# Corner weights multiplied into gathered rows: VectorE instructions of 128 elements in place of 384

## The chip, the cores and the metric

The kernel runs on one core of one Trainium2 chip. The metric is the device time of one execution in microseconds (us). The kernel before took 9420.3 us, the median of 3 runs (9414.35 to 9424.11).

## The reference, cut to what matters

Eight images of 56 x 56 places with 128 channels go through two layers. The first is a deformable convolution: for every place, 4 channel groups and 9 taps, a bilinear sample of the projected image is read at a place that depends on the data. Four corners are each multiplied by a weight, and the taps are added up:

```
def corner(yf, xf, wgt):
    valid = (yf >= 0) & (yf < H) & (xf >= 0) & (xf < W)
    idx = jnp.clip(yf, 0, H - 1).astype(jnp.int32) * W + jnp.clip(xf, 0, W - 1).astype(jnp.int32)
    v = jax.vmap(lambda im, i: im[i])(img, idx)
    return v * (wgt * valid)[..., None]
...
samp = samp.reshape(N, GROUP, H, W, P, Cg)
return jnp.einsum('nghwpc,nhwgp->nhwgc', samp, mask_sm).reshape(N, H, W, C)
```

A projection, two layer norms and an MLP follow. The second layer is an attention with additive scores, `sum(tanh(f_i + g_j + b1) * w2)`, over all earlier places j of each place i, and then a mixture of 64 experts, each of which takes 8 tokens of an image. Everything is float32.

## The kernel before

**Tiling.** An image has 3136 places. They are sampled in 49 tiles of 64 places. A tile uses 128 partitions: 64 places by two halves of the channel groups. A partition then holds two groups of 9 taps, 18 samples (`SAMPLES`), each of 32 channels by 4 corners, 128 float32 numbers. Two tiles make a block of 128 places, of which an image has 25, and a block goes through the projection, the MLP and the attention.

**Gathers.** GpSimd does nothing but issue the gathers. For each tile it issues 18 indirect DMAs, one for each sample (L1223); each reads 128 row numbers from the SBUF tensor `index` and fetches 128 rows of 512 bytes from the tensor `patches` in HBM into one of 4 slots of `gathered`. Before a tile's first gather it waits until the last user of the slot has been summed (`sampled`), which is the tile 4, or at an image's end 3, tiles earlier.

**Weighing and summing.** VectorE waits for a tile's 18 gathers (`gather_done`) and multiplies the slot in place by the corner weights in the step "weigh" (L1405). This step is called a train below. Then comes the step "sample", one reduction of 2304 elements into 64 (L1414), which frees the slot:

```
for lo in range(0, SAMPLES, PIECE):
    part = product[:, lo:lo + PIECE]
    v.tensor_tensor(part, part, weight[:, lo:lo + PIECE].unsqueeze(2)
                    .to_broadcast([P, PIECE, CG, 4]), ALU.mult)
settle()
```

`settle()` (L1242) is a drain of VectorE. Within a train there is none between the multiplications.

**The rest of a block.** After two tiles TensorE and VectorE turn, project and normalize the block ("mix", "mlp_out", "norm", L1271 to L1304, L1427, L1438, L1445), which ends in its keys (L1458 to L1461). ScalarE then computes the tanh of its scores (L1721), 16 rows at a time against up to 1024 earlier places. A block's tanh work grows with its number in the image. TensorE sums the scores (L1891), ScalarE takes the exponentials (L1731), VectorE masks them (L1471) and copies the turned weights (L1482). The weighing and all of this lie in one `pool_mem` tensor or in tensors of their own in SBUF.

**Order.** The order of the steps on TensorE, VectorE, ScalarE and the SP queue is written by a list scheduler when the kernel is built. It works with fixed costs of the steps (`LASTS`, in which "weigh" has 3.2), which do not depend on `PIECE`. Images overlap: the front of the next image and the attention of the present one are interleaved. The last image's order also takes in the experts' work.

Of the kernel before, what the change touches and what calls it, by code (L numbers as in the profile page):

```python
# [34 lines left out]
HID = 512  # L35
EPS = 1e-5
GATHER_SLOTS = 4
PIECE = 3
X1_SLOTS = 10
TANH_COLUMNS = 10240  # L40
PLACES = 4
# [682 lines left out]
def network(nc, io, x2_d, xln2_d, logits_d, patches_d, chosen_d, expert_d, out, images):  # L724
    with ExitStack() as ctx:
# [511 lines left out]
        def _(dve):  # L1237
            v = nc.vector

            def settle():  # L1240

                return v.drain()  # L1242
# [64 lines left out]
            def task(n, odd, name):  # L1307
# [88 lines left out]
                elif what == "weigh":  # L1396
# [5 lines left out]
                    weight = corner_w[:, g, tt].rearrange("p (j k) -> p j k", k=4)  # L1402
# [5 lines that stand above are left out]
# [764 lines left out]
```

How the kernel before makes its waits and increments, by code:

```python
            def task(n, odd, name):  # L1040
                what, i = (*name, 0)[:2]
                b = i % 2
                if what == "image_in":
                    sp.wait_ge(band_turned.sem, band_turned.free(n, i, 2))
                    sp.dma_start(x_band[:, b], io["x"][bass.ds(n * S + i * BAND, BAND), :]
                                 .rearrange("(q p) c -> p q c", p=112)).then_inc(x_band_in[b].sem, 16)
                elif what == "patches":
                    sp.wait_ge(patch_ready.sem, patch_ready.after(n, i))
                    if i < 2 and not (isinstance(n, int) and n == 0):
                        sp.wait_ge(sampled.sem, sampled.after(n - 1, -1))
# [4 lines left out]
                        return  # L1057
                    sp.dma_start(patches_d[int(odd)][i * P:i * P + patch_rows(i), :],
                                 patch[:patch_rows(i), b].rearrange("p g c k -> p (g c k)")).then_inc(patches_out[b].sem, 16)
                elif what == "x_in":
                    sp.wait_ge(mid_ready.sem, mid_ready.free(n, i, 2))
                    sp.dma_start(x_tok[:blk_rows(i), b], io["x"][bass.ds(n * S + i * P, blk_rows(i)), :])\
                        .then_inc(x_tok_in[b].sem, 16)
                elif what == "route":
                    r = blk_rows(i)
                    sp.wait_ge(ln2_ready.sem, ln2_ready.after(n, i))
                    sp.dma_start(x2_d[bass.ds(n * S + i * P, r), :], x2[:r, b]).then_inc(block_out[b].sem, 16)
```

## Time and profile before

| | |
|---|---|
| median of 3 runs | 9420.3 us (9414.35 to 9424.11) |
| span of the profiled execution, first to last instruction | 9429.1 us |
| mean granted TensorE clock | 0.821 of full speed |
| GpSimd busy | 6834.3 us, 7060 instructions |
| ScalarE busy | 6717.5 us, 8200 instructions |
| TensorE matmul busy | 6306.7 us |
| VectorE busy | 6031.0 us, 17780 instructions |
| multiplications by corner weights (L1405) | 2352 instructions, 1141.7 us busy |

Busy time counts an engine's compute instructions alone, so time in which GpSimd's sequencer prepares the next gather is not in it. PE is TensorE, PEld its weight loads, DVE VectorE, ACT ScalarE, POOL GpSimd; a q behind a name means the engine's sequencer (waits, drains, semaphores). A shape such as 128x384 is partitions by elements. The span of the profiled execution is 8.8 us (0.09%) above the median of the runs.

### The profile page before, as it was taken

How to read it: one execution, taken by the hardware profiler on the slowest of the kernel's cores; microseconds unless marked ns; L12 is line 12 of the kernel's file. 1: busy time of each engine (PE TensorE's matmuls, PEld its weight loads, DVE VectorE, ACT ScalarE, POOL GpSimd, SP SyncE). 2: the span in 40 equal slices, each digit the busy share in tenths (PEclk: the TensorE clock that was granted, in tenths of full speed). 3: DMA queues.
4: the chain of work that ended last, by engine and by line, in shares of the span. 5: the costliest groups of instructions: out<-in, count | busy, mean ns of one | idle time of the engine just before them, and what ended most of it. 6: DMA issues, size and time to landing. Idle time of an engine off the chain costs nothing.

```text
span 9429.1 us, 151169 instructions
## 1 busy us (share of the span) xinstructions
PE 6306.7 (67%) x44945; PEld 3370.3 (36%) x44945; DVE 6031.0 (64%) x17780; ACT 6717.5 (71%) x8200; POOL 6834.3 (72%) x7060
## 2 busy tenths in 40 slices
PE   5556666667766767666666676666676666657786
PEld 3233333333333333333333333333333333333444
DVE  6666666665676666766666666666567666776642
ACT  1368965688756887578866798567875688757891
POOL 5777777777777777777777777777777777777730
PEclk7678887888878888788888888878888888878896
DMA  2222222222222222222222222222222222334535
GB/s 86 70 76 57 58 60 63 84 58 58 62 71 76 58 59 62 74 73 57 59 63 78 67 57 62 62 83 60 57 62 69 78 57 69 97 95 134 151 111 187
DMA packets 453930, 711.90 MB, mean 75 GB/s; under 512 B 146576, under 2 KB 261136, under 8 KB 451472
## 3 DMA queue, kind: packets, MB, share of 16 engines
q0 software_dynamic: 225792, 462.87, 18.4%
q1 hardware_dynamic: 227312, 239.17, 8.0%
q8 instruction: 377, 6.18, 0.3%
q14 instruction: 449, 3.68, 0.1%
HBM read 595.51 MB, written 105.96 MB: 74 GB/s over the span
## 4 chain that ended last, share of the span: by engine, by line
POOL 66%; issue 22%; ACT 4%; DVE 3%; PE 2%; DMA 2%; DVEq 1%; SPq 0%; POOLq 0%; ACTq 0%
POOL pool_mem L1223 66%; ACT tanh L1721 3%; DVE pool_mem L1405 1%; DVEq L1242 1%; PE score_ps L1891 1%; DVE y L1414 1%; PE side_ps L2003 0%; DMA pool_mem<-in_weight 0%; DMA pool_mem<-patches_odd,pool_mem 0%; DMA pool_mem<-patches_even,pool_mem 0%; ACT expo L1731 0%; DMA expert_d<-pool_mem 0%; DVE newton L1276 0%; DVE pool_mem L1337 0%; SPq L1174 0%
## 5 line engine op out<-in xcount | busy, mean ns | idle before, releaser
L1721 ACT ACTIVATE tanh<-key_rep,query 128x896 f32<-128x896 f32 (+7 forms) x6400 | 5530.0, 951 | 1457.6 <-DVEq L1242 978.6
L1223 POOL DMA_INDIRECT pool_mem<-patches_even,pool_mem x3528 | 3414.7, 968 | 1146.5 <-issue 1072.4
L1223 POOL DMA_INDIRECT pool_mem<-patches_odd,pool_mem x3528 | 3419.4, 969 | 1075.7 <-issue 1071.7
L1891 PE MATMUL score_ps<-tanh,score_w 128*32 128x512 f32 (+3 forms) x24320 | 2931.5, 596 | 478.2 <-ACT tanh L1721 474.6
L1405 DVE TENSOR_TENSOR pool_mem<-pool_mem 128x384 f32<-128x384 f32 x2352 | 1141.7, 553 | 1334.3 <-DMA pool_mem<-patches_even,pool_mem 699.2
L1891 PEld LDWEIGHTS score_ps<-tanh,score_w 128*32 128x32 f32 x24320 | 745.9, 120 | 2087.2 <-issue 1386.1
L1414 DVE TENSOR_REDUCE y<-pool_mem 128x64 f32<-128x2304 f32 x392 | 999.6, 2550 | 33.1 <-issue 9.8
L1920 PE MATMUL value_ps<-values,expoT 128*128 128x129 f32 (+1 forms) x5200 | 908.4, 324 | 83.9 <-DVE expoT L1482 71.9
L1920 PEld LDWEIGHTS value_ps<-values,expoT 128*128 128x128 f32 (+1 forms) x5200 | 802.3, 228 | 160.7 <-DVE expoT L1482 100.7
L1276 DVE SCALAR_TENSOR_TENSOR newton<-rstd,newton 128x1 f32<-128x1 f32 (+1 forms) x2403 | 529.2, 220 | 188.1 <-issue 9.8
L1790 PE MATMUL turn_ps<-ident,expo 128*128 128x128 f32 (+1 forms) x2632 | 527.6, 323 | 152.7 <-DVE expoT L1482 128.3
L1482 DVE COPY expoT<-turn_ps 128x512 f32<-128x512 f32 (+4 forms) x800 | 455.8, 571 | 201.1 <-PE turn_ps L1790 116.0
L1731 ACT ACTIVATE expo<-score_ps,tiny 128x896 f32<-128x896 f32 (+9 forms) x416 | 383.0, 921 | 276.5 <-PE score_ps L1891 249.1
L1790 PE MATMUL chain_ps<-ident,values 128*128 128x128 f32 (+1 forms) x200 | 79.3, 396 | 730.2 <-DVE values L1445 729.4
L1278 DVE SCALAR_TENSOR_TENSOR rstd<-newton,rstd 128x1 f32<-128x1 f32 (+1 forms) x2403 | 387.8, 161 | 216.4 <-issue 26.7
L1790 PEld LDWEIGHTS turn_ps<-ident,expo 128*128 128x128 f32 (+1 forms) x2632 | 369.5, 168 | 257.1 <-DVE expoT L1482 141.6
L1821 PE MATMUL side_ps<-pool_mem,early 128*128 128x448 f32 x1008 | 427.7, 581 | 30.1 <-DVEq L1242 30.1
L1731 ACT ACT_TABLE_LOAD x198 | 254.0, 1283 | 223.8 <-PE score_ps L1891 218.6
L1867 PE MATMUL chain_ps<-w_fc,hid 128*128 128x128 f32 (+1 forms) x1600 | 250.0, 304 | 163.6 <-ACT hid L1706 163.3
L1860 PE MATMUL chain_ps<-chainT,w_fc 128*128 128x128 f32 (+1 forms) x1600 | 269.3, 320 | 119.4 <-DVE chainT L1433 117.5
L1706 ACT ACTIVATE hid<-chain_ps,b_hid 128x128 f32<-128x128 f32 (+1 forms) x800 | 226.4, 365 | 166.5 <-PE chain_ps L1860 158.4
L1790 PEld LDWEIGHTS chain_ps<-ident,values 128*128 128x128 f32 (+1 forms) x200 | 32.2, 161 | 847.6 <-DVE values L1445 815.7
(168 smaller groups left out, 6035.9 us busy)
## 6 DMA issues: line engine op xcount, KB each, us to landing
pool_mem<-in_weight SPq DMA_DIRECT2D x64, 1024.0 KB, 8.9
pool_mem<-patches_even,pool_mem POOLq DMA_INDIRECT x3528
pool_mem<-patches_odd,pool_mem POOLq DMA_INDIRECT x3528
patches_even<-pool_mem SPq DMA_DIRECT2D x104, 256.0 KB, 2.0
patches_odd<-pool_mem SPq DMA_DIRECT2D x104, 256.0 KB
pool_mem<-in_x SPq DMA_DIRECT2D x56, 224.0 KB
x_tok<-in_x SPq DMA_DIRECT2D x192, 64.0 KB
x_d<-x SPq DMA_DIRECT2D x192, 64.0 KB
```

What stands on the lines that cost most here:

```text
L1223: pool.indirect_dma_start(gathered[:, b, j * 4 * CG:(j + 1) * 4 * CG], None, patches_flat[int(odd)], bass.IndirectOffsetOnAxis(ap=index[:, ...
L1276: v.scalar_tensor_tensor(newton[:r, 1:2], rstd[:r], rstd[:r], newton[:r, 0:1], ALU.mult, ALU.mult)
L1278: v.scalar_tensor_tensor(rstd[:r], newton[:r, 1:2], 1.5, rstd[:r], ALU.add, ALU.mult)
L1405: v.tensor_tensor(part, part, weight[:, lo:lo + PIECE].unsqueeze(2) .to_broadcast([P, PIECE, CG, 4]), ALU.mult)
L1414: v.tensor_reduce(y[:, i // 2 % 2, b].rearrange("p (g c) -> p g c", c=CG), product.rearrange("p (g t) c k -> p g c t k", g=2), AX_XY, ALU. ...
L1482: last = v.tensor_copy(expoT[:rows_, pi % 2, z[0]:z[1], :r], turn_ps[:rows_, z[0]:z[1], :r])
L1721: nc.scalar.activation(tanh[:, TANH_AT[ui][0]:TANH_AT[ui][1]], key_rep[:, lo:lo + w], ACT.Tanh, bias=query[:, col:col + 1]).then_inc(tanh_ ...
L1731: nc.scalar.activation(expo[:r, ci % 2, :w], score_ps[:r, ci % 2, :w], ACT.Exp, bias=tiny[:r, 2:3])\
L1790: return mm(out, src, ident[:r, :r], is_transpose=True, start=True, stop=True)
L1821: last = mm(side_ps[:, :BAND], taps[:, t], x_pad[:, i * BAND_ROWS + dy:(i + 1) * BAND_ROWS + dy, dx:dx + W], start=t == 0, stop=t == TAPS - 1)
L1891: last = mm(score_ps[32 * col:32 * col + 32, ci % 2, lo:hi], score_w[:, place], tanh[:, TANH_AT[ui][0] + lo:TANH_AT[ui][0] + hi], start=pl ...
L1920: last = mm(value_ps[:r, :C + 1], expoT[:wj, pi % 2, z, :r], values[:wj, value_place(odd, j)], start=j == 0, stop=j == k)
```

## The change

The constant `PIECE` goes from 3 to 1. A train becomes 18 multiplications of 128 elements for each partition (one tap each) in place of 6 of 384. The products, their places, the semaphores, the drain behind the train and the order of all steps stay.

```
 GATHER_SLOTS = 4
-PIECE = 3
+PIECE = 1
 X1_SLOTS = 10
```

## Rows read from the trace of the kernel before

**Rows 1.** The page's head and its busy times by engine.
```profile
span 9429.1 us, 151169 instructions
...
PE 6306.7 (67%) x44945; PEld 3370.3 (36%) x44945; DVE 6031.0 (64%) x17780; ACT 6717.5 (71%) x8200; POOL 6834.3 (72%) x7060
```

**Rows 2.** The chain that ended last, share of the span by engine.
```profile
POOL 66%; issue 22%; ACT 4%; DVE 3%; PE 2%; DMA 2%; DVEq 1%; SPq 0%; POOLq 0%; ACTq 0%
```

**Rows 3.** GpSimd's waits: line, releaser, us in total, times, longest us.
```profile
POOL pool_mem L1223 <- issue: 2144.1, 7032, 0.3
POOL pool_mem L1223 <- DVEq L1242: 71.1, 1, 71.1
POOL pool_mem L1223 <- DVE y L1414: 7.0, 23, 0.3
```

**Rows 4.** Gathers (L1223) by source line: duration ns min/median/max, first and last start us.
```profile
L1223 POOL DMA_INDIRECT pool_mem<-patches_even,pool_mem x3528: 941/947/1335, 71.5 to 7928.8; - x196
L1223 POOL DMA_INDIRECT pool_mem<-patches_odd,pool_mem x3528: 941/947/1431, 1195.7 to 9055.8; - x196
```

**Rows 5.** Groups of instructions: busy us, mean ns of one, idle before.
```profile
L1223 POOL DMA_INDIRECT pool_mem<-patches_odd,pool_mem x3528 | 3419.4, 969 | 1075.7 <-issue 1071.7 <-DVE y L1414 4.0
L1223 POOL DMA_INDIRECT pool_mem<-patches_even,pool_mem x3528 | 3414.7, 968 | 1146.5 <-issue 1072.4 <-DVEq L1242 71.1 <-DVE y L1414 3.0
L1405 DVE TENSOR_TENSOR pool_mem<-pool_mem 128x384 f32<-128x384 f32 x2352 | 1141.7, 553 | 1334.3 <-DMA pool_mem<-patches_even,pool_mem 699.2 <-DMA pool_mem<-patches_odd,pool_mem 626.6 <-issue 2.4
```

**Rows 6.** Timeline, one train and the gathers beside it: start us, us.
```profile
4014.86 0.95 POOL L1223 DMA_INDIRECT pool_mem<-patches_odd,pool_mem  x1 [0.30 <-issue]
4014.91 2.90 DVE L1405 TENSOR_TENSOR pool_mem<-pool_mem 128x384 f32<-128x384 f32 x6 [4.78 <-DMA pool_mem<-patches_odd,pool_mem]
...
4016.11 1.11 POOL L1223 DMA_INDIRECT pool_mem<-patches_odd,pool_mem  x1 [0.30 <-issue]
...
4017.53 1.10 POOL L1223 DMA_INDIRECT pool_mem<-patches_odd,pool_mem  x1 [0.30 <-issue]
...
4018.94 0.95 POOL L1223 DMA_INDIRECT pool_mem<-patches_odd,pool_mem  x1 [0.30 <-issue]
```

**Rows 7.** Timeline of GpSimd, two later trains' gathers, start 4038.67 and 4060.59.
```profile
4038.97 1.08 POOL L1223 DMA_INDIRECT pool_mem<-patches_odd,pool_mem  x1 [0.30 <-issue]
4040.35 1.10 POOL L1223 DMA_INDIRECT pool_mem<-patches_odd,pool_mem  x1 [0.30 <-issue]
...
4060.64 1.33 POOL L1223 DMA_INDIRECT pool_mem<-patches_odd,pool_mem  x1 [0.30 <-issue]
4062.28 1.10 POOL L1223 DMA_INDIRECT pool_mem<-patches_odd,pool_mem  x1 [0.30 <-issue]
4063.68 0.94 POOL L1223 DMA_INDIRECT pool_mem<-patches_odd,pool_mem  x1 [0.30 <-issue]
4064.93 0.95 POOL L1223 DMA_INDIRECT pool_mem<-patches_odd,pool_mem  x1 [0.31 <-issue]
4066.18 0.95 POOL L1223 DMA_INDIRECT pool_mem<-patches_odd,pool_mem  x1 [0.30 <-issue]
```

**Rows 8.** Timeline of VectorE: those two trains and the sum behind the second.
```profile
4038.67 2.90 DVE L1405 TENSOR_TENSOR pool_mem<-pool_mem 128x384 f32<-128x384 f32 x6
...
4060.59 2.90 DVE L1405 TENSOR_TENSOR pool_mem<-pool_mem 128x384 f32<-128x384 f32 x6 [4.38 <-DMA pool_mem<-patches_odd,pool_mem]
4063.73 0.69 DVE L1337 COPY pool_mem<-side_ps 128x512 f32<-128x512 f32 x1 [0.24 <-issue]
4064.56 2.55 DVE L1414 TENSOR_REDUCE y<-pool_mem 128x64 f32<-128x2304 f32 x1
```

**Rows 9.** Timeline of VectorE: multiplication of 128 elements, two SBUF inputs (L1471).
```profile
4055.48 0.28 DVE L1471 TENSOR_TENSOR expo<-expo,earlier 128x128 f32<-128x128 f32 x1
4055.68 0.28 DVE L1433 COPY chainT<-chain_ps 128x128 f32<-128x128 f32 x1
```

**Rows 10.** Timeline of GpSimd, the gather that began beside it and the next.
```profile
4055.53 1.05 POOL L1223 DMA_INDIRECT pool_mem<-patches_odd,pool_mem  x1 [0.30 <-issue]
4056.89 0.95 POOL L1223 DMA_INDIRECT pool_mem<-patches_odd,pool_mem  x1 [0.30 <-issue]
```

**Rows 11.** Windows by stage: us, busy (x) of each engine, PEclk, DMA share, GB/s.
```profile
3440.00:4563.00 1123.00, 754.93 (x5316) 397.55 (x5312) 729.72 (x2180) 836.27 (x1022) 854.09 (x883) 0.82 0.24 65
...
7933.00:8644.00 711.00, 468.77 (x3461) 260.43 (x3454) 515.53 (x1453) 490.94 (x611) 541.77 (x556) 0.80 0.36 101
8644.00:9057.00 413.00, 318.47 (x2836) 170.29 (x2835) 262.26 (x758) 365.97 (x423) 313.97 (x325) 0.90 0.47 138
9057.00:9429.00 372.00, 285.32 (x2079) 175.73 (x2078) 123.28 (x307) 164.76 (x184) 0.00 (x0) 0.76 0.52 164
```

**Rows 12.** The chain where it leaves GpSimd: start us, us, what.
```profile
8643.90 5.89 DMA pool_mem<-patches_odd,pool_mem
8649.81 0.56 DVE pool_mem L1405
...
8666.79 13.16 ACT tanh L1721 x14
```

**Rows 13.** ScalarE's longest waits, us in total, times, longest us.
```profile
ACT tanh L1721 <- DVEq L1242: 978.6, 83, 26.2
ACT tanh L1721 <- PE score_ps L1891: 474.5, 136, 18.2
```

## The prediction

> **What bounds the kernel now.** I read the page's busy times first [rows 1]. Four engines stand between 64% and 72%, and none looks like the bound. The chain that ended last says otherwise: 66% of the span is GpSimd in its gathers and 22% is "issue" [rows 2]. The waits of GpSimd explain this [rows 3]. It waits once, 71.1 us at the start, for the first indices. After that every gather is preceded by 0.3 us that nothing outside explains, and even the 23 times put down to the sum L1414 are no longer than 0.3. So from 71.5 us, when the first gather starts, to 9057 us, about 1 us after the last one starts [rows 4], GpSimd issues 7056 gathers without a gap. A gather takes 968.5 ns on average [rows 5] and 0.305 us lies between two, and 7056 x 1.2735 = 8986 us, which is the distance from 71.5 to 9057. An image is 1123 us of this stream, a tile 8986 / 392 = 22.92 us.
>
> The stream does not set the end to the last gather. The chain leaves GpSimd at 8644 us in the last image and goes on through one train into tanh [rows 12]. By then (8644 - 71.5) / 22.92 = 374 of the 392 tiles have been gathered. From there ScalarE is busy 366 of 413 us, while it was busy 836 of 1123 in an image of the middle [rows 11]: the late blocks of an image carry more tanh than two tiles' gathers cover, and in the last image nothing comes behind to make up for it. What shortens a gather before 8644 us shortens the kernel by as much; what shortens one behind it does little.
>
> **Why gathers touch the change.** The median gather takes 947 ns, the mean 968.5, the longest 1431 [rows 4, 5]. The timeline shows where the long ones are. At 4014.91 a train starts; the gather that started just ahead of it takes 0.95 us, the two that start during it 1.11 and 1.10, the next 0.95 again [rows 6]. Two later trains do the same, with 1.08 and 1.10, then 1.33 and 1.10 [rows 7, 8]. Gathers that start during the sum L1414, which has one input, take 0.95 [rows 7, 8]. A multiplication of 128x128 elsewhere in the kernel, which also has two inputs in SBUF, does it too: it starts at 4055.48, the gather that starts at 4055.53 takes 1.05, the next one 0.95 [rows 9, 10].
>
> The sizes fit one reading: a gather needs, right at its start, something that a two-input instruction holds until near its end. For 384 elements: train at 4060.59, gather at 4060.64, wait 1.33 - 0.95 = 0.38, so it is released 0.43 us after the instruction's start. For 128 elements: 0.05 + (1.05 - 0.95) = 0.15 us after the start. The difference is 0.28 us for 256 elements. The Trainium skill, page "SBUF — State Buffer", section "Who interferes with whom", gives a rule for this: a VectorE instruction with two SBUF inputs contends with a GpSimd instruction that reads SBUF, and the loser blocks for the whole instruction. The trace agrees, 0.38 us against 384 elements and 0.10 against 128.
>
> **Removed: long holds.** Six instructions of 0.55 us make a train of 2.90 us, so they follow each other every (2.90 - 0.55) / 5 = 0.47 us. Of these the hold is about 0.41 and the rest, about 0.06, is free. A gather released at the end of a hold starts its successor 0.947 + 0.305 = 1.25 us later, which is 2.66 spacings. It lands inside another hold with 0.155 us to go, so gathers lock to 1.10 us, which is what most rows show. The price of a train now is 0.31, 0.28 and 0.53 us in the three shown. The mean over the whole kernel has the upper bound (968.5 - 947) x 7056 / 392 = 0.39 us, if all excess were put on the trains; the multiplications elsewhere, as at 4055.53, take some of it. I take 0.34, bounds 0.28 and 0.39.
>
> **Added: short holds, more of them.** No row shows a train of 128-element instructions. The next instruction behind the one at 4055.48 starts 0.20 us later [rows 9], and 0.47 less 256 elements (0.28 by the release times, 0.27 by the durations, 0.55 - 0.28) is 0.19 to 0.20. I take 0.20. A train is then 17 x 0.20 + 0.28 = 3.7 us, of which 3.5 are at risk, and 3.5 / 1.25 = 2.8 gathers start in it. The hold is about 0.15 - 0.02 = 0.13 us of each 0.20, and a gather at a random phase waits 0.13 x 0.13 / (2 x 0.20) = 0.042 us. That is 2.8 x 0.042 = 0.12 us for a train. It hangs on the phase. 1.25 / 0.20 is 6.25 spacings, so the successor of a released gather comes 0.05 us behind the end of a hold, within the free 0.07, and waits for nothing; the one after it misses the free part. The lower bound is 0.04, one short wait. The upper one is 0.27, with two waits of 0.13. I take 0.12.
>
> Saving on the path: 374 x (0.34 - 0.12) = 82 us. The bounds are 374 x (0.39 - 0.04) = 131 and 374 x (0.28 - 0.27) = 4; with the middle value of either side, 374 x (0.34 - 0.27) = 26 and 374 x (0.34 - 0.04) = 112.
>
> **Added: VectorE time.** 12 more instructions in each of 392 trains. A train is 3.7 - 2.9 = 0.8 us longer, 314 us in all: L1405 goes from 1141.7 us to about 1455, VectorE from 6031 to about 6345 us, 64% to 68%. The cover is the gather stream. VectorE idles 1326 us ahead of L1405 for gathers that have not landed [rows 5]. A slot is needed again two or three tiles after its last gather, 46 to 69 us, and a train (3.7) with its sum (2.6) ends well within that; GpSimd has never waited for one [rows 3]. If the cover were gone, all 314 us would be on the path. On the path today is the one train at 8649.81 [rows 12], so 0.8 us. Behind it 18 trains in the last image run beside a ScalarE that is 89% busy. If each delayed it by its full 0.8 it would be 14 us, if none, nothing. I take 4, nearer to nothing, because tanh has its own backlog there. Each chain step that VectorE runs behind a train (the norms, keys, copies of turned weights) starts 0.8 us later too. ScalarE waits 978.6 us for keys [rows 13] in phases in which it has nothing else, and before 8644 us that is not on the path.
>
> The Trainium skill, page "VectorE: DVE Perf Modes", section "The TRN2 errata — SBUF-src ops pay a fixed extra latency per instruction", speaks against the change: each instruction pays a fixed latency, many small tiles pay it each time, and tiles of 512 elements or more are advised. Its table's 58 fixed cycles at 0.96 GHz would make an estimate of 0.06 us for each of the 4704 added instructions, 284 us of VectorE time. The trace agrees on the size, (0.20 x 3 - 0.47) / 2 = 0.065 us each, but shows that time off the path.
>
> **Sum.** Against the profiled execution: 9429.1 - 82 + 0.8 + 4 = 9352. The runs' median is 8.8 below the span, so 9343 us.
>
> **The rivals.**
> - *Bad phase.* If the hold is a little longer than 0.13 or the spacing under 0.20, the free part is missed and a train costs 0.27: 9420 - 26 + 5 = 9399 us. Against it stand 0.28 and 0.20 in rows 9, for it that only one row has the 128-element release. Chance 0.10.
> - *The port is not given back between instructions of a train.* Gathers wait as now, each for about as long as now, and more of them meet the longer train. The change would not do what it is cut for; the gain is nothing, 9420 + 5 = about 9425 us. Against it: the gather at 4060.64 was released at 0.43 us, the end of the first of six instructions, not at the end of the train. Chance 0.04.
> - *Slower: the gathers lock to full waits.* If the remainder of 1.25 us over the spacing falls just behind the free part (spacing of 0.196: remainder 0.074), every one of three gathers waits 0.13, 0.39 for a train. With 14 us from the end of the last image this is 9420 + 374 x 0.05 + 14 = 9453 us. It decides when the spacing lies within some 0.002 us of that value. Chance 0.04.
> - *Slower: VectorE becomes the bound.* If the added time delays each slot's release to GpSimd, it is 9420 - 82 + 314 = 9652 us. It decides where a sum ends later than two tiles (46 us) after its gathers, and nothing in rows 3 is near that. The page that advises large tiles would give this. Chance 0.03.
>
> **How the numbers follow.** The forecast, with its own range of 9310 (saving 112) to 9385, has the rest, 0.79. Two executions are told apart by about 0.2%, 19 us. Faster by more than that are the forecast and four fifths of the bad phase, 0.87; within it the rest of the bad phase and the second rival, 0.06; slower 0.07. The range takes in the bad phase, 9300 to 9400.
>
> **What the profile after would show.** L1405 has 7056 instructions of some 0.28 us and about 1455 us busy. The mean gather falls from 968.5 to about 956 ns, since (0.34 - 0.12) x 392 / 7056 = 0.012 us. Gathers beside a train take 0.95 to 1.08 and none 1.33. The median stays 947, and the 0.3 us of issue stays. The image's period falls from 1123 to about 1112 us. Waits of GpSimd for L1414 stay at 0.3 us at most. The prediction is wrong if gathers beside trains still take 1.10, if a GpSimd wait over 0.3 us appears, or if the time from the point where the chain leaves GpSimd to the end grows by more than 15 us.

## The result and the profile after

The changed kernel takes 9604.5 us, the median of 4 runs (9598.8 to 9628.7), against 9422.2 us for the kernel before in the same session (9414.4 to 9427.4). The ratio is 1.0198, with a 95% interval of 1.0186 to 1.021: 182 us slower, where 77 us faster was forecast, and 204 us above the forecast's upper end.

The head, the busy times, the chain and the two groups that matter, from the page of the kernel after. They answer to [rows 1, 2, 5].

```profile
span 9606.8 us, 155873 instructions
...
PE 6353.2 (66%) x44945; PEld 3379.6 (35%) x44945; DVE 6372.4 (66%) x22484; ACT 6720.4 (70%) x8200; POOL 7019.1 (73%) x7060
...
POOL 70%; issue 22%; ACT 3%; PE 2%; DMA 1%; DVE 1%; SPq 0%; POOLq 0%; DVEq 0%; ACTq 0%
...
L1223 POOL DMA_INDIRECT pool_mem<-patches_even,pool_mem x3528 | 3504.0, 993 | 1148.5 <-issue 1075.2
L1223 POOL DMA_INDIRECT pool_mem<-patches_odd,pool_mem x3528 | 3514.9, 996 | 1075.8 <-issue 1075.8
...
L1405 DVE TENSOR_TENSOR pool_mem<-pool_mem 128x128 f32<-128x128 f32 x7056 | 1479.5, 285 | 1190.9 <-DMA pool_mem<-patches_even,pool_mem 632.0
```

The span grew by 177.7 us and GpSimd's busy time by 7019.1 - 6834.3 = 184.8 us, for the same 7060 instructions. Nothing else of this size stands on the path. VectorE's busy time grew by 341 us, the multiplications' by 337.8 (1479.5 against 1141.7), so one may suspect that VectorE now holds the kernel up. GpSimd's waits decide that (line, releaser, us in total, times, longest us); they answer to [rows 3].

```profile
POOL pool_mem L1223 <- issue: 2151.0, 7054, 0.3
POOL pool_mem L1223 <- DVEq L1242: 73.0, 1, 73.0
POOL pool_mem L1223 <- DVE y L1414: 0.3, 1, 0.3
```

It waits for a sum once, for 0.3 us. The stream of gathers still has no gap: from 73.5 to about 9243.7 us (last start 9242.7, below) is 9170 us, 23.39 us for a tile where it was 22.92. To tile 374, where the prediction took the stream to leave the path, that makes 374 x 0.47 = 176 us. What lies behind that tile takes 9606.8 - (73.5 + 374 x 23.39) = 785 us, and took 785. (The chain itself now leaves GpSimd later, at 8908.7 us, 698 us before the end.) The whole loss is in the duration of the gathers. The gathers by source line (duration ns min/median/max), against [rows 4]:

```profile
L1223 POOL DMA_INDIRECT pool_mem<-patches_even,pool_mem x3528: 943/947/3925, 73.5 to 8088.6; - x196
L1223 POOL DMA_INDIRECT pool_mem<-patches_odd,pool_mem x3528: 943/947/3820, 1229.1 to 9242.7; - x196
```

The median is the old one, 947 ns. The mean went from 968.5 to 994.7 ns, and the longest from 1431 to 3925. So a few gathers take far longer. The timeline of GpSimd beside three trains (start us, us):

```profile
4007.91 1.01 POOL L1223 DMA_INDIRECT pool_mem<-patches_odd,pool_mem  x1 [0.30 <-issue]
4009.23 2.53 POOL L1223 DMA_INDIRECT pool_mem<-patches_odd,pool_mem  x1 [0.31 <-issue]
4012.06 0.94 POOL L1223 DMA_INDIRECT pool_mem<-patches_odd,pool_mem  x1 [0.30 <-issue]
...
4033.33 0.96 POOL L1223 DMA_INDIRECT pool_mem<-patches_odd,pool_mem  x1 [0.30 <-issue]
4034.60 2.12 POOL L1223 DMA_INDIRECT pool_mem<-patches_odd,pool_mem  x1 [0.31 <-issue]
...
4057.04 2.11 POOL L1223 DMA_INDIRECT pool_mem<-patches_odd,pool_mem  x1 [0.30 <-issue]
4059.46 0.95 POOL L1223 DMA_INDIRECT pool_mem<-patches_odd,pool_mem  x1 [0.30 <-issue]
```

and of VectorE, whose trains they are:

```profile
4007.21 3.72 DVE L1405 TENSOR_TENSOR pool_mem<-pool_mem 128x128 f32<-128x128 f32 x18 [2.63 <-DMA pool_mem<-patches_odd,pool_mem]
...
4032.17 3.73 DVE L1405 TENSOR_TENSOR pool_mem<-pool_mem 128x128 f32<-128x128 f32 x18 [2.55 <-DMA pool_mem<-patches_odd,pool_mem]
...
4054.58 3.75 DVE L1405 TENSOR_TENSOR pool_mem<-pool_mem 128x128 f32<-128x128 f32 x18 [0.99 <-DMA pool_mem<-patches_odd,pool_mem]
```

The first gather of the first train comes 0.70 us into it and waits 1.01 - 0.95 = 0.06 us, the short wait of the prediction. The next one, 2.02 us in, takes 2.53. Read it from its end. Without a wait it would need 0.95 us, so it was released at 4009.23 + 2.53 - 0.95 = 4010.81. The last of the 18 multiplications starts 0.28 us before the train's end, at 4010.65, so the release is 0.16 us into the last one. The other two come out the same: released at 4035.77 and 4058.20, with last multiplications at 4035.62 and 4058.05. These gathers waited until the train was in its last multiplication, over five to eight boundaries between instructions. I call that a stall. All 183 gathers beside trains that waited for more than one spacing of the multiplications (0.202 us) were released in the same place, 0.15 to 0.17 us behind the start of the last of the 18.

Counted over all records of both traces: before, 1086 gathers waited, for 157.7 us together. After, 453 gathers waited for less than one spacing of the multiplications, 27.9 us together, and 211 for longer, 316.2 us together. That is 344 - 158 = +186 us, the +184.8 of GpSimd. Of the 211, 28 started beside other instructions with two inputs (9 us together, as much as before). The 183 beside trains make up 308 us, the short waits beside trains 10 us. Before, the waits beside trains were 132 us.

### The profile page after: what moved, and what is told of

It reads as the page before. It is cut to its first block, busy times and chain, and to the rows that moved or that the text cites. A ratio compares the mean times of both kernels' runs of the same rounds, so it can differ in the third digit from the quotient of the medians.

```text
span 9606.8 us, 155873 instructions
## 1 busy us (share of the span) xinstructions
PE 6353.2 (66%) x44945; PEld 3379.6 (35%) x44945; DVE 6372.4 (66%) x22484; ACT 6720.4 (70%) x8200; POOL 7019.1 (73%) x7060
## 4 chain that ended last, share of the span: by engine, by line
POOL 70%; issue 22%; ACT 3%; PE 2%; DMA 1%; DVE 1%; SPq 0%; POOLq 0%; DVEq 0%; ACTq 0%
POOL pool_mem L1223 70%; ACT tanh L1721 3%; PE side_ps L2003 0%; PE score_ps L1891 0%; DMA pool_mem<-in_weight 0%; DMA expert_d<-pool_mem 0%; ACT expo L1731 0%; DMA out_x<-pool_mem 0%; DVEq L1242 0%; DVE pool_mem L1405 0%; PE score_ps L1952 0%; DVE pool_mem L1337 0%; PE score_ps L1790 0%; PE score_ps L2057 0%; SPq L1174 0%
## 5 line engine op out<-in xcount | busy, mean ns | idle before, releaser
L1223 POOL DMA_INDIRECT pool_mem<-patches_even,pool_mem x3528 | 3504.0, 993 | 1148.5 <-issue 1075.2
L1223 POOL DMA_INDIRECT pool_mem<-patches_odd,pool_mem x3528 | 3514.9, 996 | 1075.8 <-issue 1075.8
L1405 DVE TENSOR_TENSOR pool_mem<-pool_mem 128x128 f32<-128x128 f32 x7056 | 1479.5, 285 | 1190.9 <-DMA pool_mem<-patches_even,pool_mem 632.0
L1843 PE MATMUL chain_ps<-ident,y 64*64 64x64 f32 x1200 | 158.4, 262 | 274.3 <-DVE y L1414 201.5
```

The source lines that it names most:

```text
L1223: pool.indirect_dma_start(gathered[:, b, j * 4 * CG:(j + 1) * 4 * CG], None, patches_flat[int(odd)], bass.IndirectOffsetOnAxis(ap=index[:, ...
```

## The experiments

Three theories were told apart; the expectations speak of them in these or like words.
- **Time**: the added VectorE time (drains included) is what costs, by whichever wait.
- **Phase**: a gather loses only because its successor, 1.25 us later, falls again into a hold. Then a spacing (the time from the start of one multiplication to the next) with another remainder cures it.
- **Row**: in a long unbroken row of short multiplications the gather is no longer let in between two of them, and waits for the row's end. Then a drain inside the row cures it, though it costs VectorE time.

On three of the chips used, the kernel before took 14,589 to 14,621 us in place of 9,420. All variants of the whole kernel below ran on these, but for drain3_d. In their traces GpSimd waits more than 5,200 us for sums, and a tile's train starts some 105 to 110 us after its last gather (1.6 us in the trace before), though the gather's own packets move 1.2 us behind it as ever. So it is not the gathers that come late there, as the expectation of drain3_b has it, but VectorE, and the times tell nothing of a gapless gather stream. Only the single gathers beside trains are read. GpSimd's waits in e144:

```profile
POOL pool_mem L1223 <- DVE y L1415: 5263.3, 305, 38.8
POOL pool_mem L1223 <- issue: 2058.7, 6750, 1.2
```

### Other sizes of a multiplication: e144 and e192

The train is cut across the channels, 16 x 144 elements, and in 12 of 3 taps by 16 channels, 192 elements.

```diff
-for lo in range(0, SAMPLES, PIECE):
-    part = product[:, lo:lo + PIECE]
+for lo in range(0, SAMPLES, 18):            # e192: (0, SAMPLES, 3)
+    for at in range(0, CG, 2):              # e192: (0, CG, 16)
+        part = product[:, lo:lo + 18, at:at + 2]
```

> The train is 16 multiplications of 144 elements (18 taps by 2 channels) in place of 18 of 128, so nearly as many, nearly as short, and as long in all. Only the spacing changes, from 0.202 to about 0.219 us. Phase theory: a gather that has waited is followed 1.251 us later by one that arrives 0.156 us behind the end of a hold (1.251 less 5 spacings), in the middle of the next hold, and not in the last 0.02 us before an instruction's start. No gather then takes over 1.2 us, each waits about 0.06 us, a train costs about 0.2 us and the kernel takes about 9365 us (9345 to 9400). Row theory (a long row of short instructions starves GpSimd whatever the phase): stalls as with PIECE = 1, about 9580 to 9620 us. Time theory (VectorE's 0.8 us more for each train is what costs): about 9600 us.

> The train is 12 multiplications of 192 elements (3 taps by 16 channels), spacing about 0.269 us. Phase theory: the gather behind one that waited arrives 0.175 us behind the end of a hold of some 0.2 us, so in a hold, with about 0.09 us to go: no stalls, some 0.25 us for each train, about 9390 us (9370 to 9410). Row theory: a row of 12 is still long, stalls of 1 us and more, 9480 to 9600 us. Time theory: trains are 3.3 us, 0.4 longer than with PIECE = 3, so about 9500 us.

e144 took 14642.0 us, ratio 1.0014 (0.9996 to 1.0032); e192 14618.0, ratio 1.0005 (0.9988 to 1.0021). In e144 107 gathers waited longer than one spacing (91 of them beside trains), 144 us together, the longest gather 3792 ns; in e192 82 (73 beside trains), 91 us, longest 3526. In e144 52 of the 54 gathers that came right behind one with a short wait, in a row that no earlier gather had delayed, stalled, though its spacing leaves another remainder of 1.25 us: they came 0.11 us behind the start of a multiplication, in the changed kernel 0.196. Phase alone falls. The timeline of one train of e144:

```profile
4126.35 3.58 DVE L1406 TENSOR_TENSOR pool_mem<-pool_mem 128x144 f32<-128x144 f32 x16
4127.25 3.49 POOL L1223 DMA_INDIRECT pool_mem<-patches_even,pool_mem  x1 [0.30 <-issue]
...
4131.05 0.94 POOL L1223 DMA_INDIRECT pool_mem<-patches_even,pool_mem  x1 [0.30 <-issue]
```

The gather of 3.49 us is the first of its train and was released at 4127.25 + 3.49 - 0.95 = 4129.79, again just behind the start of the last multiplication, some 0.3 us before 4129.93. A gather ahead that waited is no condition.

### A drain every third multiplication, and more time without it: drain3, longer

drain3 is the changed kernel with a drain behind every third multiplication; longer is the kernel before with two small statistics instructions of 128 elements, each with its drain, behind the train.

```diff
 for lo in range(0, SAMPLES, 1):
     ...
+    if lo % 3 == 2:
+        settle()
```
```diff
 settle()
+for _ in range(2):
+    v.bn_stats(bst[:], ident[:])
+    settle()
```

> PIECE = 1 with a drain behind every third multiplication, so that a row is 3 instructions and not 18; the train grows to about 4.6 us. Phase theory and row theory alike: a stalled gather is released at the next drain, at most 0.6 us later, so no gather over 1.7 us, the 183 long ones shrink to 0.3 us of excess each, and the kernel takes 9340 to 9400 us. Time theory: VectorE has 1.7 us more for each train than with PIECE = 3, so 9700 us or more.

> PIECE = 3 with two single-input instructions of 128 elements and their drains behind each train (bn_stats of ident into a scratch tile), about 0.75 us more of VectorE time before each sum, and no more holds. Time theory: about 9600 us. Phase theory and row theory: 9420 to 9435 us, with GpSimd's waits as before.

drain3 took 14982.3 us, ratio 1.024 (1.0202 to 1.0278), longer 14818.9, ratio 1.0133 (1.0096 to 1.0171). Where GpSimd waits for VectorE, as on these chips, added work with drains does cost. (Multiplications alone cost little there: e144 adds 0.68 us to a train as well, and 22 us in all.) The gathers tell more: drain3's mean is 948 ns and its longest 1432, and no gather beside a train stalled. Both were repeated on another such chip, and drain3 once more on a third, with the same outcome: drain3_b 14963.0 us, 1.0256 (1.0239 to 1.0273); longer_b 14763.8, 1.0123 (1.0106 to 1.014); drain3_c 14981.5, 1.0239 (1.0206 to 1.0271).

The trains of longer and longer_b are those of the kernel before, six multiplications of 384 elements, and were to show no stall. Two gathers of longer and three of longer_b stalled all the same, for 2.53 to 2.68 us, each as the first gather of its train. GpSimd and VectorE of longer:

```profile
6818.80 2.68 POOL L1223 DMA_INDIRECT pool_mem<-patches_odd,pool_mem  x1 [0.30 <-issue]
```
```profile
6817.76 2.89 DVE L1405 TENSOR_TENSOR pool_mem<-pool_mem 128x384 f32<-128x384 f32 x6
```

The release, 6818.80 + 2.68 - 0.95 = 6820.53, is 0.43 us into the sixth multiplication. All five had started 1.0 to 1.2 us into their train, where the two runs have 29 gathers. The trace before has 100 such gathers, and none stalled.

> PIECE = 1 with a drain behind every third multiplication; on the chip of the first group, whose gathers landed some 100 us late, no gather beside a train took over 1.5 us, but the time there told nothing. Row theory (a gather is stalled only where VectorE has run three or more two-input instructions in a row undisturbed): no stall here, about 0.04 us for each train in place of 0.34, so GpSimd's stream is 110 us shorter than before; 1.7 us more VectorE time for each train costs up to 30 us in the last image: 9310 to 9345 us. Time theory (the added VectorE time is what made PIECE = 1 slow): 1.7 us for each train, twice that of PIECE = 1, so about 9780 us.

> PIECE = 3 with two single-input instructions and their drains behind each train, 0.75 us more VectorE time for each train as with PIECE = 1, no more holds. Time theory: about 9600 us. Row theory: 9420 to 9435 us, mean gather 968 ns as before.

> PIECE = 1 with a drain behind every third multiplication, once more, on another chip. Row theory: no stall (rows of three are too short), about 0.04 us for each train in place of 0.34, so GpSimd's stream is 110 us shorter than before; the added 1.7 us of VectorE time for each train is hidden but for up to 30 us in the last image: 9310 to 9345 us where before takes 9422. Time theory (the added VectorE time is what made PIECE = 1 slow): about 9780 us.

### The length of the row: piece2 and drain6

piece2 has `PIECE = 2`, nine multiplications of 256 elements. drain6 is the changed kernel with a drain behind every sixth (`lo % 6 == 5`).

> PIECE = 2: rows of 9 multiplications of 256 elements, spacing about 0.335 us, a train of 3.1 us. Row theory: from the fourth on a gather can be stalled to the end of the train, at most 1.7 us; about a third of the trains stalled by 1 us each, and short waits of some 0.15 us: 0.4 to 0.5 us for each train, 9430 to 9500 us, between PIECE = 3 and PIECE = 1. If instead the stalls belong to the 128-element size, there are none and it takes 9360 to 9390 us. Time theory: 0.2 us more for each train, about 9460 us.

> PIECE = 1 with a drain behind every sixth multiplication, 2 drains more in a train (3 with the last), train 4.1 us. Row theory: stalls begin at the fourth of a row and end with the row, so at most 0.5 us each and in a fifth of the arrivals there; 0.08 us for each train, 9320 to 9350 us. If rows of six were as bad as rows of 18, gathers over 1.2 us would be as many as with PIECE = 1 (211). Time theory: 1.2 us for each train, about 9690 us.

piece2 took 14658.7 us, ratio 1.0047 (1.003 to 1.0064), drain6 14850.0, 1.0182 (1.0165 to 1.0199). Stalls beside trains: 10 in piece2 (longest gather 3103 ns), 14 of 338 in drain6 (longest 1696 ns, bounded by its short rows; one is over the spacing by 1 ns only). Counted by how many multiplications of its row had started before the gather did (gathers ahead of the row's last multiplication, in rows of which no earlier gather had delayed any):

| multiplications started | after (18 x 128) | drain6 (3 x 6 x 128) | piece2 (9 x 256) | before (6 x 384) |
|---|---|---|---|---|
| 1 to 3 | 0 of 131 stalled | 1 of 140 | 7 of 89, all at 3 | 0 of 338 |
| 4 and 5 | 11 of 53 | 13 of 69 | 3 of 31, all at 4 | 0 of 120 |
| 6 | 15 of 151 | no such | 0 of 19 | no such |
| 7 to 9 | 56 of 65 | no such | 0 of 32 | no such |
| 10 to 13 | 94 of 117 | no such | no such | no such |

At 128 elements the stalls set in at the third or fourth multiplication, and behind six or more most gathers stall. This is the row theory, but with 256 elements the stalls keep to the start of the row (none of the 72 gathers at 5 or more), which it does not explain, and longer has them at the third of six at 384. The changed kernel shows one more condition. Where an earlier gather of the same train had pushed the next multiplication back by some 0.04 us, 7 of 326 gathers stalled.

The table leaves a rival open, since nearly every gather of its last two lines also came at one phase, in the last 0.02 us ahead of the next multiplication. The same trace tells the two apart: of the gathers at that phase 0 of 16 stalled at 1 to 3, 7 of 53 at 4 to 6, and 146 of 178 at 7 to 13. So the place in the row counts. The size of a multiplication counts too. Of the gathers that came right behind one with a short wait in a row not delayed, these stalled:

| elements | run | phase behind a start, of the spacing, us | stalled |
|---|---|---|---|
| 128 | after | 0.196 of 0.202 | 131 of 131 |
| 144 | e144 | 0.110 of 0.219 | 52 of 54 |
| 192 | e192 | 0.131 of 0.269 | 50 of 85 |
| 256 | piece2 | 0.199 of 0.335 | 0 of 65 |
| 384 | before | 0.271 of 0.469 | 0 of 113 |

### The train and the gathers alone: m3, m1, m1one, m1d3

To be rid of the other engines, four kernels leave out everything but gathers (rows of x by constant indices), multiplications (by 0.5) and sums, and hand back a copy of x: 392 tiles of 18 gathers, 4 slots. m3 multiplies 6 x 384 elements, m1 18 x 128, m1one puts 18 statistics instructions of 128 elements in their place, which have one input, m1d3 is m1 with a drain every third. Ahead of every second train stand up to seven small statistics instructions, so that trains and gathers meet at many offsets.

```diff
-v.tensor_tensor(part, part, weight[:, lo:lo + PIECE]..., ALU.mult)
+v.bn_stats(bst[:, 6 * lo:6 * lo + 6], gathered[:, b, lo * 4 * CG:(lo + 1) * 4 * CG])   # m1one
```

> Gathers, multiplications and sums alone (392 tiles of 18 gathers, weights 0.5, the output is a copy of x; in every second tile 0 to 7 small instructions stand ahead of the train, so that the phase varies). 6 multiplications of 384. GpSimd's stream sets the time: 7056 x 0.947 + 7056 x 0.305 = 8834 us if nothing waited, and about 0.3 us for each train on top, so 8950 to 9000 us with some 30 us around it. All theories say so.

> The same with 18 multiplications of 128. Row theory: 100 to 250 gathers of 1.2 to 3.9 us, mean gather 0.985 to 1.0 us, 100 to 220 us slower than m3. Time theory (VectorE's added time, or work that hangs on it): VectorE is idle most of the time here, so the added 0.8 us is hidden, and with the short waits alone it would be 50 to 110 us faster than m3, as predicted for the whole kernel.

> 18 instructions of 128 elements with one input (bn_stats of the gathered rows into a scratch tile) in place of the multiplications: as many instructions, about as long a train, no second input. Row theory and lock: no gather over 1.0 us, 8834 us and what lies around it. If the number of VectorE instructions starved GpSimd, long gathers would be there as in m1.

> 18 multiplications of 128 with a drain behind every third. Row theory: no gather over 1.25 us, mean gather about 0.950 us, 8850 to 8880 us, about 100 us faster than m3. If the row's length did not matter, stalls as in m1.

Medians: m3 9873.5 us, m1 9928.0, m1one 9903.7, m1d3 9915.8. All four miss what was expected (m3 by 870 us; m1 was to be 100 to 220 us slower than m3 and is 54). They settle little. They ran on a chip on which the kernel before takes 14,618 us, and in m1, m1one and m1d3 VectorE stands idle in the middle of a train, up to 1.1 us between two of a row and 11 us at one place in m1; GpSimd waited 729 us for sums in m1 and 904 in m1one. Gathers of 1.5 to 1.81 us are in all four, 314 of them in m3, 118 of these beside no multiplication at all; what makes these is not known. Over 1.85 us are 73 in m1 and none in the other three.

### The same in a loop: n3, n1, n1one, n1d3

The same four as a loop over four tiles, with three or five statistics instructions ahead of every second train. These ran on a chip on which the kernel before takes 9,420 us, so it is not told apart whether the loop or the chip rid them of the idle times.

```diff
-for t in range(TILES):
-    b = t % SLOTS
+with dve.Fori(0, TILES // SLOTS) as n:
+    for b in range(SLOTS):
```

> Gathers, multiplications and sums alone, in a loop of 4 tiles: 6 multiplications of 384. If the loop keeps VectorE and GpSimd fed, the stream sets the time, 8950 to 9100 us. All theories say so; it is the base of the other three.

> The same with 18 multiplications of 128. Row theory: 100 to 250 gathers over 1.8 us, released at the end of the train, 100 to 250 us slower than n3. Lock theory as predicted for the kernel (short holds, short waits): no such gather and 50 to 110 us faster than n3. If VectorE's rows are still broken by late instructions, fewer long gathers and no clear difference.

> 18 single-input instructions of 128 in place of the multiplications. Row theory and lock theory: no gather that ends with the train, 8840 to 8950 us, at least 80 us under n3. If VectorE's instruction count starved GpSimd: as n1.

> 18 multiplications of 128 with a drain behind every third. Row theory: no gather over 1.3 us beside a train, 60 to 120 us under n3. If row length did not matter: as n1.

| | us, median of 4 | less n3 | mean gather, ns | longest, ns | gathers over 1.8 us |
|---|---|---|---|---|---|
| n3, 6 x 384 | 8976.4 (8976.1 to 8977.1) | | 965 | 1332 | 0 |
| n1, 18 x 128 | 9122.3 (9115.1 to 9141.7) | +146 | 985 | 3322 | 153 |
| n1one, 18 with one input | 8825.8 (8824.3 to 8826.0) | -151 | 944 | 1080 | 0 |
| n1d3, drain every third | 8897.8 (8897.2 to 8898.6) | -79 | 954 | 1080 | 0 |

The groups of gathers, one line of each page, in the order of the table (busy us, mean ns | idle before, releasers):

```profile
L61 POOL DMA_INDIRECT gathered<-in_x,index x7056 | 6809.8, 965 | 2154.3 <-issue 2126.0
```
```profile
L61 POOL DMA_INDIRECT gathered<-in_x,index x7056 | 6948.8, 985 | 2153.7 <-issue 2153.7
```
```profile
L61 POOL DMA_INDIRECT gathered<-in_x,index x7056 | 6657.4, 944 | 2154.4 <-issue 2133.1
```
```profile
L62 POOL DMA_INDIRECT gathered<-in_x,index x7056 | 6730.0, 954 | 2154.0 <-issue 2147.6
```

The idle time is the same in all four, 0.305 us for each gather, so the stream is gapless and the kernels differ in nothing but the gathers' durations: 6948.8 - 6809.8 = 139 us of n1 over n3, beside 146 in the runs' medians. The change's loss is here without the rest of the kernel. n1one has as many VectorE instructions as n1, nearly as close (3.58 us for 18, against 3.72), and is the fastest: the number of instructions is not the cause. But its instructions also write 6 numbers in place of 128, so n1one alone does not tell the second input from the output. The trace before does. The addition L1300 has 128 elements, one input in PSUM and one in SBUF, and writes to SBUF:

```profile
592.16 0.28 DVE L1300 TENSOR_TENSOR biased<-chain_ps,rows 128x128 f32<-128x128 f32 x1
```
```profile
592.21 0.94 POOL L1223 DMA_INDIRECT pool_mem<-patches_even,pool_mem  x1 [0.30 <-issue]
```

None of the 36 gathers that started in it with over 0.15 us to go waited for more than 0.02 us. Of those in the addition L1304, of the same size with both inputs in SBUF, 38 of 43 did. So it is the second SBUF input. n1d3 has more VectorE time than n1 (a train of 4.56 us) and is 225 us faster. Time falls. Row stands, with the limits that the two tables above set. In n1, stalls make up 278 us and short waits 11; n3 has 150 us, all short.

Two trains of n1, one with a stall and one without:

```profile
4014.14 3.72 DVE L85 TENSOR_TENSOR gathered<-gathered,weight 128x128 f32<-128x128 f32 x18
4014.84 1.02 POOL L61 DMA_INDIRECT gathered<-in_x,index  x1 [0.30 <-issue]
4016.16 2.53 POOL L61 DMA_INDIRECT gathered<-in_x,index  x1 [0.30 <-issue]
...
4036.47 0.94 POOL L61 DMA_INDIRECT gathered<-in_x,index  x1 [0.30 <-issue]
4036.49 3.80 DVE L85 TENSOR_TENSOR gathered<-gathered,weight 128x128 f32<-128x128 f32 x18 [16.00 <-DMA gathered<-in_x,index]
4037.72 0.94 POOL L61 DMA_INDIRECT gathered<-in_x,index  x1 [0.30 <-issue]
4038.96 0.94 POOL L61 DMA_INDIRECT gathered<-in_x,index  x1 [0.30 <-issue]
```

In the second the gathers get in first, take their 0.94 us, and it is the train that gives way: 3.80 us in place of 3.72, some 0.04 us for each of two gathers. In the first a gather waited 0.08 us and its successor lost until the train's end. 130 of 134 such successors in n1 (in rows not delayed) stalled.

### The cure in the whole kernel: drain3_d

The same edit as drain3, on a chip on which the kernel before takes 9420.9 us.

> The whole kernel with PIECE = 1 and a drain behind every third multiplication. In the loops this kept half of the excess over single-input instructions (72 of 150 us) and no stall. Row theory: GpSimd's stream is 75 to 110 us shorter than before; the added 1.7 us of VectorE time for each train is hidden but for up to 30 us in the last image: 9320 to 9370 us where before takes 9420, and no gather over 1.5 us. Time theory (VectorE's added time is what made PIECE = 1 slow): about 9780 us.

It takes 9368.8 us (9368.4 to 9371.5), ratio 0.9945 (0.9928 to 0.9961): 52 us faster than the kernel before and 236 faster than the change without drains. From its page and its gathers by source line:

```profile
span 9369.6 us, 157833 instructions
...
PE 6293.4 (67%) x44945; PEld 3342.6 (36%) x44945; DVE 6535.4 (70%) x22484; ACT 6718.5 (72%) x8200; POOL 6762.3 (72%) x7060
...
L1405 DVE TENSOR_TENSOR pool_mem<-pool_mem 128x128 f32<-128x128 f32 x7056 | 1647.0, 289 | 787.6 <-DMA pool_mem<-patches_even,pool_mem 329.8
```
```profile
L1223 POOL DMA_INDIRECT pool_mem<-patches_even,pool_mem x3528: 940/944/1200, 72.0 to 7867.6; - x196
L1223 POOL DMA_INDIRECT pool_mem<-patches_odd,pool_mem x3528: 940/944/1452, 1183.7 to 8983.3; - x196
```

And one of its trains with its gathers:

```profile
4005.99 4.55 DVE L1405 TENSOR_TENSOR pool_mem<-pool_mem 128x128 f32<-128x128 f32 x18
4006.05 1.04 POOL L1223 DMA_INDIRECT pool_mem<-patches_odd,pool_mem  x1 [0.30 <-issue]
4007.40 0.94 POOL L1223 DMA_INDIRECT pool_mem<-patches_odd,pool_mem  x1 [0.30 <-issue]
4008.65 0.95 POOL L1223 DMA_INDIRECT pool_mem<-patches_odd,pool_mem  x1 [0.30 <-issue]
4009.91 1.04 POOL L1223 DMA_INDIRECT pool_mem<-patches_odd,pool_mem  x1 [0.31 <-issue]
```

The train is 0.83 us longer than the changed kernel's and 1.65 longer than before's, VectorE is 504 us busier than before, and GpSimd is 72 us less busy. The gathers that meet a train wait 0.14 us at most, 0.19 us for a train in all where it was 0.34. Of the 72 us some 55 are shorter waits; the rest is mostly the gather that does not wait, 944 ns here at the median and 947 before, which differs as much between other runs (their shortest gathers take 938 to 943 ns) and is not put down to the drains. The stream runs from 72.0 to 8984.3 us, 22.735 us for a tile, and by tile 374 is 374 x (22.923 - 22.735) = 70 us ahead of the kernel before. What lies behind that tile takes 9369.6 - (72.0 + 374 x 22.735) = 795 us in place of 785, so some 10 us are given back: the chain leaves GpSimd earlier, at 8028 us, and goes on mostly through tanh.

## Why the prediction was wrong

**What bounds the kernel: right.** The stream is still gapless after the change, and its length explains 176 of the 178 us. The part behind tile 374 was forecast 4.8 us longer and came out as long as before.

**VectorE's time: right.** 0.28 us each, a spacing of (3.72 - 0.28) / 17 = 0.202 for the forecast 0.20, 1479.5 us for the forecast 1455, and hidden: GpSimd's longest wait for a sum is 0.3 us. The fourth rival, VectorE as the bound at 9652 us, lay nearest to the result and is refuted; had it been nearer still, that would have been luck. n1one and drain3_d show the same from the other side.

**Removed, long holds: right.** The 384-element trains cost 0.34 us each, counted beside trains, as forecast.

**Added, short holds: the step that failed.** It took it that every boundary between two multiplications lets a waiting gather in, so that "a gather at a random phase waits 0.13 x 0.13 / (2 x 0.20) = 0.042 us" and a train costs 0.12 us, and that "gathers beside a train take 0.95 to 1.08". For the short waits that was even too dear: the 146 beside trains are 10 us over 392 trains, 0.03 each. But 183 gathers were let in at no boundary before the last multiplication, and their 308 us are 0.79 us a train. The prediction also had the successor of a released gather fall "within the free 0.07", where it "waits for nothing". It did fall there, 0.19 to 0.20 us behind the start of a multiplication, and all 131 that did in a row not delayed stalled. The step rested on one release, the gather at 4060.64 [rows 7], let in behind the first of six instructions of 384, and on a lone 128-element multiplication [rows 9, 10]. Neither is a row of eighteen short ones, and the text did not bound its cost by the worst case, a wait until the row's end. Such a bound can be worked out from the rows, as an estimate: a gather starts every 1.25 us, so the first in a train comes some 0.6 us into it, and let in only at the last multiplication, at 17 x 0.20 + 0.15 = 3.55 us, it waits 2.95 us, which is 374 x (2.95 - 0.34) = 976 us slower.

**The rivals.** The second one, "the port is not given back between instructions of a train", named what happens, with a chance of 0.04, and dismissed it by the same gather at 4060.64. It also had the wrong price, since it let each gather wait "for about as long as now". Had it asked how long a gather waits that is not let in before the train's end, it would have been a rival on the slower side. Priced now from the trace after: 374 tiles by 0.47 us, 9596 us. The gathers that lock to full waits of 0.13 us (9453 us) did not come about, as the short waits were fewer than before.

The Trainium skill, page "SBUF — State Buffer", section "Who interferes with whom", says that the shared read access is held for one instruction and that the one who issues second blocks until the first is through. The trace before agrees: a wait of 0.38 us beside a first instruction of 0.55. The trace after shows more than the rule: in rows of 128 elements the second one blocks over up to 15 instructions (a gather of 3925 ns, a wait of 2.98 us). The same section says that a VectorE instruction with at most one SBUF input, outside the modes that use both port pairs, does not contend. n1one agrees, with no gather above 1080 ns, and so does L1300.

**The advice for large tiles**, which the prediction took from the Trainium skill, page "VectorE: DVE Perf Modes", section "The TRN2 errata — SBUF-src ops pay a fixed extra latency per instruction", spoke against the change for its fixed cost per instruction. That cost is here, (3 x 0.202 - 0.47) / 2 = 0.07 us each, and hidden. The change lost for another reason.

**What stays open.** Shown is that the loss is the stalls, that the instructions beside them have two SBUF inputs, that at 128 elements rows of six and more have stalls and rows of three none, and that a stall ends in the row's last multiplication or at a drain. Not shown is the mechanism: why a gather keeps losing for the rest of the row, why this grows rare from 128 to 256 elements, why the stalls there stop behind the fourth multiplication, why at 384 only five were seen, all on chips on which the kernel takes 14,600 us, and why a row that an earlier gather has pushed by 0.04 us is nearly free of them. No trace records the port itself.

## What to carry to other kernels

Where GpSimd issues gathers without a gap, a row of two-input VectorE instructions beside it is a cost to the gathers, and its pieces are not independent: look for the longest gather, not only the mean, in the trace of any new shape. Break a row of short ones with a drain behind every third instruction if VectorE has time to spare (here 0.83 us a train bought 236 us); on the chips on which GpSimd waited for VectorE the same drains cost 2.4%. An operation with one SBUF input can cost the gathers nothing, but look at the one that you use: beside the statistics instructions, the sums and L1300 no gather waited, while in the trace before 17 of the 73 that started beside the 128-element tensor_scalar L1445 or L1504, which read one tensor and two columns of scalars from SBUF, waited 0.02 to 0.06 us. When a rival is dismissed by one row, price it at its worst from that row all the same, and see whether the row has the shape of the change.

## What was unexpected of the hardware

- A gather of 0.95 us took up to 3.9 us beside a row of 128-element multiplications. Each gather that got in first delayed the row by some 0.04 us.
- More instructions and more drains made the kernel faster: 504 us more VectorE time, 52 us less in all.
- The same kernel took 9,420 us on some chips and 14,600 on others, with runs on each within 1% of one another. On the latter VectorE stood idle inside some rows of multiplications (up to 3.9 us between two in drain3), and the profile names no other engine for it. The cause was not looked into.
